# FFN rows split into fp16 halves in row layout and transposed by DMA instead of by TensorE

## The chip, the cores and the metric

One core of a Trainium2 chip runs the kernel. The metric is device time in microseconds, the median of several executions; the time before is 355.26 us (3 runs, 355.12 to 355.71). TensorE (PE) multiplies and, with an identity as the other operand, transposes 128x128 blocks into PSUM; VectorE (DVE), ScalarE (ACT) and GpSimd (POOL) do the element-wise work; SyncE (SP) only issues DMAs here.

## The reference, cut to what matters

`x`, `cond` and `ctx` are 8 items of 256 rows of 256 numbers (`cond` one row per item). First comes a slot attention of three rounds, then the feed-forward part (FFN) that the change is in. Everything is float32.

```python
x = x + xcond(cond, ctx, layernorm(x), ...)      # keys and values from ctx, 3 rounds of
                                                 # attention + MLP over 256 slots
x = x + ffn(layernorm(x), W_fc, ln_w, ln_b, W_proj)

def ffn(x, W_fc, ln_w, ln_b, W_proj):            # W_fc (1024, 256), W_proj (256, 1024)
    h = einsum('btd,hd->bth', x, ternary(W_fc))  # ternary: -1, 0 or 1 per weight
    h = gelu(h)
    h = (h - mean(h)) * rsqrt(var(h) + 1e-5) * ln_w + ln_b
    return einsum('bth,dh->btd', h, ternary(W_proj))
```

## The kernel before

All data stay in SBUF after the loads at the start. Each engine runs its own instruction stream, written out by hand; they meet at semaphores, and a waiting instruction holds all behind it on its engine. The first part prepares keys and values (up to about 50 us), the second is the three rounds (to about 280 us, the FFN's first items enter near its end), the third is the FFN, 8 items (b = 0 to 7) of two row tiles of 128 rows (rt = 0, 1); r = 2b + rt numbers the 16 row tiles. A buffer for items has two slots, u = b % 2.

The ternary weights are exact in fp16, and the other operand is split into a high fp16 half and the rest, a low fp16 half; both are multiplied, so a product costs two fp16 passes instead of a float32 one. The path of an item b through the FFN, with the functions' names:

- `stats_f` (DVE, `BATCH_NORM_STATS2` and `AGGREGATE`, L304 and L312) and `ln_coef` (POOL): mean and 1/sigma of each row. `apply_f` (DVE, L770): the normalised rows into `XR`, a part of the tile `PR`, float32, 128 partitions x (2 row tiles x 256).
- `rows_t` (PE, L351): four 128x128 transposes of `XR` into `ps_t[0]`.
- `copy_high` (ACT, L566): the transposed rows to fp16, `XTh`. `low_parts` (DVE, L777): the float32 transposed rows less `XTh`, `XTl`. Both lie in the memory of the tile `V`, which the FFN reuses; so do `GTh` and `GTl`.
- `fc` (PE, L1061): first-layer products of row tile r, 8 matmuls of 512 columns into `ps_mid`; at rt = 0 it waits for `low_parts` of its item. `gelu_half` (ACT, L572, into a part of `KT`); `centre` (DVE, first L784 the mean, then L790 two halves); `square_half` (ACT, L580); `rstd_g` (POOL).
- `hidden_t` (PE, L1075): eight transposes of the centred hidden row tile into `ps_low`; `high_half` (ACT, L587) and `low_half` (DVE, L799) split them; `proj` (PE, L1085): second-layer products, 16 matmuls of 256 columns into `ps_t`; `result` (DVE, L807): scale and add to `X`. The store (SP, L401) follows when both row tiles of the item are done.

The steps are shifted against each other. While PE does `fc` of row tile r it does `hidden_t` of r-1 and `proj` of r-2 right behind it: in item b, at rt = 0, the order is `fc(2b)`, `hidden_t(2b-1)`, `rows_t(b+1)`, `proj(2b-2)`; at rt = 1 `fc(2b+1)`, `hidden_t(2b)`, `proj(2b-1)`. DVE's order at rt = 0 is `stats_f(b+2)`, `centre(2b)`, `result(2b-2)`, `low_half(2b-1)`, `low_parts(b+1)`, and at rt = 1 `centre(2b+1)`, `result(2b-1)`, `low_half(2b)`, `apply_f(b+2)`. ACT's at rt = 0 is two gelus, two `high_half`, two squares, `copy_high(b+1)`.

Of the kernel before, what the change touches and what calls it, by code (L numbers as in the profile page):

```python
# [27 lines left out]
P = 128  # L28
# [28 lines left out]
def build(nc, x, ctx_in, w_nat, w_tr, w_fc_t, w_proj_t, cols, rows, out):  # L57
    with ExitStack() as stack:
# [67 lines left out]
        XR = PR[:, 0:2]  # L126
        vf = V[:, :, :, :].rearrange("p b j d -> p (b j d)")
# [10 lines left out]
        XTh = halves(0, 2 * C2 * N).rearrange("p (u c k) -> p u c k", u=2, c=C2)  # L138
        XTl = halves(C2 * N, 2 * C2 * N).rearrange("p (u c k) -> p u c k", u=2, c=C2)
# [70 lines left out]
        xth_ready = sem("xth_ready")  # L210
        xtl_ready = sem("xtl_ready")
# [79 lines left out]
        def ring(t, half, b):  # L291

            return t * STEPS + (B + half * B + b)

# [83 lines left out]
        @block.sync  # L378
        def _(sp):
            def load(dst, src, s, b):  # L380
                if b >= 2:
                    sp.wait_ge(s[b % 2], 16 * (b // 2))
                sp.dma_start(flat(dst, b), src[b]).then_inc(s[b % 2], 16)


            load(S, c_v, ctx_in_sem, 0)
            load(S, c_v, ctx_in_sem, 1)
            sp.wait_ge(wk_in, 16)
            for b in range(B):
                load(X, x_v, x_in_sem, b)  # L390
                if b + 2 < B:
                    load(S, c_v, ctx_in_sem, b + 2)
            sp.dma_start(wn[:, W1:W2 + 1].rearrange("p w c d -> p w (c d)"),
                         w_nat[3:5].rearrange("w p n -> p w n")).then_inc(mlp_in, 16)
            sp.dma_start(rowv[:, ROWS_EARLY:], rows[ROWS_EARLY:].rearrange("(a n) -> a n", a=1)
                         .broadcast_to([P, NROW - ROWS_EARLY])).then_inc(rows_in, 16)
            sp.dma_start(wf[:, 0:C2 * H], w_fc_t).then_inc(ffn_in, 16)
            sp.dma_start(wf[:, C2 * H:], w_proj_t).then_inc(ffn_in, 16)
            with sp.Fori(0, B) as b:
                sp.wait_ge(o_done, 2 * b + 2)  # L400
                sp.dma_start(o_v[b], flat(X, b)).then_inc(stored, 16)  # L401
            sp.wait_ge(stored, 16 * B)
# [118 lines left out]
        def _(act):  # L521
# [40 lines left out]
            def copy_high(b, u):  # L562
                act.wait_ge(t_ready, b + (T_FFN + 1))
                if not early(b):
                    act.wait_ge(f1_ready, 4 * b - 4)
                act.activation(XTh[:, u].rearrange("p c k -> p (c k)"), ps_t[0][:], ACT.Copy).then_inc(xth_ready, 1)  # L566
# [101 lines left out]
        def _(dve):  # L668
# [96 lines left out]
            def apply_f(b, u):  # L765
                dve.wait_ge(lnf.coef, b + 1)
                if not early(b):
                    dve.wait_ge(t_ready, b + (T_FFN - 1))  # L768
# [4 lines left out]
            def low_parts(b, u):  # L773
                dve.wait_ge(xth_ready, b + 1)
                if not early(b):
                    dve.wait_ge(f1_ready, 4 * b - 4)
                dve.tensor_tensor(XTl[:, u].rearrange("p c k -> p (c k)"), ps_t[0][:],  # L777
                                  XTh[:, u].rearrange("p c k -> p (c k)"), ALU.subtract).then_inc(xtl_ready, 1)
# [199 lines left out]
        def _(pe):  # L978
# [64 lines left out]
            def rows_t(b, u):  # L1043
                pe.wait_ge(xf_ready, 2 * b + 2)
                if isinstance(b, int) and b == 0:
                    pe.wait_ge(t_copied, T_FFN + RING)
                else:
                    pe.wait_ge(xtl_ready, b)
                blocks_t(pe, ps_t[0], XR[:, u])

            def fc(b, u, r, rt):
                if rt == 0:
                    pe.wait_ge(xtl_ready, b + 1)
                for h in range(2):
# [5 lines left out]
                    for k, (c, part) in enumerate(parts):  # L1060
                        last = pe.matmul(ps_mid[h][:], part[:, u, c, rt * P:(rt + 1) * P],  # L1061
# [27 lines left out]
            def ffn(b, u, rt, last=None):  # L1089
# [5 lines left out]
                if rt == 0 and (last is None or last < B - 1):  # L1095
                    rows_t(b + 1, 1 - u)
# [3 lines left out]
            def into_ffn(s):  # L1100
# [12 lines left out]
                if s == STEPS - 1:  # L1113
                    rows_t(0, 0)
# [87 lines left out]
```

## Time and profile before

| | |
|---|---|
| median of 3 runs | 355.26 us |
| profiled execution, span | 353.3 us |
| PE busy | 318.4 us (90%), of weights' loads 259.6 us beside it |
| DVE busy | 280.1 us (79%) |
| ACT busy | 241.1 us (68%) |
| POOL busy | 242.3 us (69%) |
| DMA | 13.20 MB, nearly all in the first 40 us |

The profile gives the profiled execution by its span, 353.3 us, and no other time of its own; what the median has more, 1.96 us, lies around the span. PE's matmuls are pipelined, so each group's listed time is some 0.16 us longer than the distance to the next group. Of the chain of waits that ended last, the FFN's PE lines are the largest parts (L1085 3%, L1061 2%); it reaches back to 319 us only. The FFN's items follow each other every 9.54 us in the steady part.

### The profile page before, as it was taken

Reading aid. Unit: us, or ns where it says so; the run is one execution under the profiler, and the core shown is the slowest. Engines: PE = TensorE matmul, PEld = TensorE weight load, DVE = VectorE, ACT = ScalarE, POOL = GpSimd, SP = SyncE. Lnnn points to the kernel's source line nnn. Section 1 sums busy time; section 2 is a strip of 40 time slices with the busy share of each in tenths; the row PEclk is TensorE's granted clock in tenths of the full one; section 3 lists DMA queues with packets and bytes.
Section 4 is the critical chain, followed back from the end, with each engine's and each line's share of the span. In section 5 each row is a group of like instructions: output and inputs, shape, how many; then the busy total and the mean of one; then the engine's idle time right before and its main releaser. Section 6 shows DMA issues by size and latency. Waiting matters only on the chain. (4 is left out here: it accounts for less than half of the span.)

```text
span 353.3 us, 7208 instructions
## 1 busy us (share of the span) xinstructions
PE 318.4 (90%) x1758; PEld 259.6 (73%) x1758; DVE 280.1 (79%) x849; ACT 241.1 (68%) x563; POOL 242.3 (69%) x529
## 2 busy tenths in 40 slices
PE   7997799999898888998989788999997599999995
PEld 7876687888786666777867676888874367777774
DVE  3699876899668779686697698896699889999874
ACT  2267786956856687757567977575548768888881
POOL 4278888267678888847688888668586985555331
PEclk9999999999999999999999999999999789999999
DMA  8997000000000000000000000000000000000001
GB/s 290 308 326 299 0 1 0 2 2 1 2 2 0 1 2 1 3 1 1 0 0 1 0 0 1 0 2 2 0 1 0 3 31 26 6 30 30 32 30 59
DMA packets 5312, 13.20 MB, mean 37 GB/s; under 512 B 673, under 2 KB 673, under 8 KB 4897
## 3 DMA queue, kind: packets, MB, share of 16 engines
q1 hardware_dynamic: 4160, 10.88, 8.6%
q10 hardware_dynamic: 1120, 1.98, 1.5%
q8 instruction: 10, 0.16, 0.2%
q14 instruction: 22, 0.17, 0.2%
HBM read 10.76 MB, written 2.10 MB: 36 GB/s over the span
## 5 line engine op out<-in xcount | busy, mean ns | idle before, releaser
L359 PE MATMUL ps_mid<-XT,wt 128*128 128x256 f32 x192 | 45.7, 381 | 2.9 <-ACT XT L370 2.9
L359 PE MATMUL ps_low<-V,PR 128*128 128x257 f32 x192 | 45.8, 381 | 0.5 <-DVE PR L882 0.5
L359 PE MATMUL ps_mid<-XT,KT 128*128 128x256 f32 x192 | 45.5, 380 | 0.6 <-ACT XT L370 0.6
L359 PE MATMUL ps_low<-wn,GT 128*128 128x256 f32 x192 | 45.2, 379 | 0.0
L335 ACT ACTIVATE XH<-S,lnp_ab 128x256 f32<-128x256 f32 x48 | 26.2, 593 | 24.0 <-POOL lnp_ab L329 23.9
L351 PE MATMUL ps_t<-ident,XH 128*128 128x128 f32 x192 | 29.7, 278 | 13.3 <-ACT XH L335 13.1
L335 ACT ACTIVATE XH<-S,lnm_ab 128x256 f32<-128x256 f32 x48 | 26.2, 595 | 22.0 <-POOL lnm_ab L329 22.0
L359 PEld LDWEIGHTS ps_low<-V,PR 128*128 128x128 f32 x192 | 36.3, 190 | 5.9 <-DVE PR L882 0.9
L359 PEld LDWEIGHTS ps_low<-wn,GT 128*128 128x128 f32 x192 | 36.4, 190 | 4.9
L359 PEld LDWEIGHTS ps_mid<-XT,wt 128*128 128x128 f32 x192 | 34.6, 190 | 7.3 <-ACT GT L650 2.3
L351 PEld LDWEIGHTS ps_t<-ident,XH 128*128 128x128 f32 x192 | 22.5, 141 | 23.2 <-ACT XH L335 12.3
L359 PEld LDWEIGHTS ps_mid<-XT,KT 128*128 128x128 f32 x192 | 34.6, 190 | 4.5 <-ACT XT L370 0.8
L370 ACT ACTIVATE XT<-ps_t 128x512 f32<-128x512 f32 x56 | 32.9, 588 | 4.4 <-PE ps_t L351 4.4
L506 POOL TENSOR_TENSOR S<-S,rowv 128x256 f32<-128x256 f32 x48 | 34.1, 732 | 0.0
L1085 PE MATMUL ps_t<-w,V 128*128 128x256 f16 x256 | 32.1, 282 | 0.9 <-DVE V L799 0.9
L1061 PE MATMUL ps_mid<-w,V 128*128 128x512 f16 x128 | 30.6, 382 | 0.8 <-ACT KT L572 0.7
L920 DVE TENSOR_TENSOR S<-ps_low,S 128x512 f32<-128x512 f32 x24 | 16.5, 687 | 18.1 <-PE ps_low L359 12.0
L1085 PEld LDWEIGHTS ps_t<-w,V 128*128 128x128 f16 x256 | 25.8, 101 | 4.6 <-DVE V L799 1.2
L790 DVE SCALAR_TENSOR_TENSOR KT<-KT,gneg,rowv 128x512 f32<-128x512 f32 x32 | 27.6, 904 | 1.0
L647 ACT ACTIVATE PR<-ps_mid,nmax 128x256 f32<-128x256 f32 x48 | 22.0, 461 | 8.4 <-DVE nmax L892 8.1
L580 ACT ACTIVATE XH<-KT,gneg 128x512 f32<-128x512 f32 x32 | 22.9, 723 | 5.2 <-DVE gneg L784 5.2
L572 ACT ACTIVATE KT<-ps_mid 128x512 f32<-128x512 f32 x32 | 19.0, 594 | 8.3 <-PE ps_mid L1061 7.2
(135 smaller groups left out, 743.4 us busy)
## 6 DMA issues: line engine op xcount, KB each, us to landing
S<-ctx SPq DMA_DIRECT2D x8, 256.0 KB, 3.8
X<-x SPq DMA_DIRECT2D x8, 256.0 KB, 3.8
out<-X SPq DMA_DIRECT2D x8, 256.0 KB, 2.0
rowv<-rows SPq DMA_DIRECT2D x1, 1920.0 KB, 9.9
wf<-w_fc_t SPq DMA_DIRECT2D x1, 1024.0 KB, 11.7
wf<-w_proj_t SPq DMA_DIRECT2D x1, 1024.0 KB, 13.6
wt<-w_tr ACTq DMA_DIRECT2D x1, 512.0 KB, 4.2
wn<-w_nat ACTq DMA_DIRECT2D x1, 512.0 KB, 5.7
```

The lines of the kernel that those rows point to most:

```text
L335: last = act.activation(dst[:, j], src[:, j], ACT.Identity, bias=ln.ab[:, at, 1, j:j + 1], scale=ln.ab[:, at, 0, j:j + 1])
L351: last = pe.transpose(dst[:, c * K + j * P:c * K + (j + 1) * P], src[:, j, c * P:(c + 1) * P], ident[:])
L359: last = pe.matmul(dst(m), lhs_t[:, c, m * P:(m + 1) * P], rhs[:, c, 0:n], start=(c == 0), stop=(c == 1))
L370: act.activation(XT[:, u].rearrange("p c k -> p (c k)"), ps_t[u][:], ACT.Copy).then_inc(t_copied, 1)
L506: pool.tensor_tensor(S[:, b, j], S[:, b, j], cond_row[:, b], ALU.add)\
L572: act.activation(Gf[:, rt, h * HALF:(h + 1) * HALF], ps_mid[h][:], ACT.Gelu, accum_out=gsum[:, rt, h:h + 1]).then_inc(gelu_done, 1)
L580: act.activation(flat(XH, 2 * rt + h), Gf[:, rt, h * HALF:(h + 1) * HALF], ACT.Square, bias=gneg[:, rt:rt + 1], accum_out=qsum[:, rt, h:h ...
L647: act.activation(dst[:, b % 4, j], src, ACT.Exp, bias=nmax[:, b, j:j + 1], accum_out=rsum[:, b, j:j + 1]).then_inc(mid_read, 1)
L790: dve.scalar_tensor_tensor(out=GC[:, rt, h * HALF:(h + 1) * HALF], in0=Gf[:, rt, h * HALF:(h + 1) * HALF], scalar=gneg[:, rt:rt + 1], in1= ...
L920: dve.tensor_tensor(flat(S, b), ps[:, 0], flat(S, b), ALU.add).then_inc(low_read, 2)
L1061: last = pe.matmul(ps_mid[h][:], part[:, u, c, rt * P:(rt + 1) * P], WfT[:, c, h * HALF:(h + 1) * HALF], start=(k == 0), stop=(k == 3))
L1085: last = pe.matmul(ps[:, 0:D], part[:, rt, k], WpT[:, k], start=(k == 0 and part is GTh), stop=(k == HT - 1 and part is GTl))
```

## The change

The split comes ahead of the transpose. `copy_high` and `low_parts` stay where they are in ACT's and DVE's order, but read the rows `XR` in SBUF and write the fp16 halves `XRh` and `XRl` in row layout (the other two quarters of `PR`). SP then issues two transposing DMAs for each item, fp16, each 128 partitions x 512 elements into 4 blocks of 128x128, straight into `XTh` and `XTl`, whose layout is now row tile, then column block. `fc` at rt = 0 waits for both (`xt_in`). `rows_t` is gone from PE. SP's loop of stores is written out, with the transposes for item b ahead of the store of item b-2.

```diff
--- before.py
+++ after.py
@@ -124,6 +124,12 @@
         GC = KT[:, :, :, :].rearrange("p b c n -> p (b c n)")[:, 2 * H:4 * H].rearrange("p (r h) -> p r h", r=2)
 
         XR = PR[:, 0:2]
+
+        def half_words(t, n):
+            return t.rearrange("p j k -> p (j k)").bitcast(F16).rearrange("p (u j d) -> p u j d", u=n, j=J2)
+
+        XRh = half_words(PR[:, 2], 2)
+        XRl = half_words(PR[:, 3], 2)
         vf = V[:, :, :, :].rearrange("p b j d -> p (b j d)")
 
         def halves(at, n):
@@ -135,8 +141,8 @@
         gneg = sb("gneg", [2])
         grstd = sb("grstd", [2, 3])
 
-        XTh = halves(0, 2 * C2 * N).rearrange("p (u c k) -> p u c k", u=2, c=C2)
-        XTl = halves(C2 * N, 2 * C2 * N).rearrange("p (u c k) -> p u c k", u=2, c=C2)
+        XTh = halves(0, 2 * C2 * N).rearrange("p (u j c k) -> p u j c k", u=2, j=J2, c=C2)
+        XTl = halves(C2 * N, 2 * C2 * N).rearrange("p (u j c k) -> p u j c k", u=2, j=J2, c=C2)
         GTh = halves(2 * C2 * N, 2 * HT * P).rearrange("p (r t k) -> p r t k", r=2, t=HT)
         GTl = halves(2 * C2 * N + HT * P, 2 * HT * P).rearrange("p (r t k) -> p r t k", r=2, t=HT)
 
@@ -207,8 +213,9 @@
         lnb_copied = sem("lnb_copied")
         x1_ready = sem("x1_ready")
         x1_shifted = sem("x1_shifted")
-        xth_ready = sem("xth_ready")
-        xtl_ready = sem("xtl_ready")
+        xrh_ready = sem("xrh_ready")
+        xrl_ready = sem("xrl_ready")
+        xt_in = [sem(f"xt_in{u}") for u in range(2)]
         f1_ready = sem("f1_ready")
         gelu_done = sem("gelu_done")
         gneg_ready = sem("gneg_ready")
@@ -291,6 +298,10 @@
         def ring(t, half, b):
 
             return t * STEPS + (B + half * B + b)
+
+        def xt_landed(b, u):
+
+            return 16 * b + (32 - 16 * u)
 
         T_FFN = B + ROUNDS * STEPS
 
@@ -396,9 +407,22 @@
                          .broadcast_to([P, NROW - ROWS_EARLY])).then_inc(rows_in, 16)
             sp.dma_start(wf[:, 0:C2 * H], w_fc_t).then_inc(ffn_in, 16)
             sp.dma_start(wf[:, C2 * H:], w_proj_t).then_inc(ffn_in, 16)
-            with sp.Fori(0, B) as b:
-                sp.wait_ge(o_done, 2 * b + 2)
-                sp.dma_start(o_v[b], flat(X, b)).then_inc(stored, 16)
+            def rows_t(b):
+                u = b % 2
+                sp.wait_ge(xrh_ready, b + 1)
+                sp.wait_ge(xrl_ready, b + 1)
+                if b >= 2:
+                    sp.wait_ge(f1_ready, 4 * b - 4)
+                for dst, src in ((XTh, XRh), (XTl, XRl)):
+                    sp.dma_start_transpose(dst[:, u].rearrange("p j c k -> p (j c) k"),
+                                           src[:, u].rearrange("p j d -> p (j d)")).then_inc(xt_in[u], 16)
+
+            for b in range(B + 2):
+                if b < B:
+                    rows_t(b)
+                if b >= 2:
+                    sp.wait_ge(o_done, 2 * b - 2)
+                    sp.dma_start(o_v[b - 2], flat(X, b - 2)).then_inc(stored, 16)
             sp.wait_ge(stored, 16 * B)
 
         @block.gpsimd
@@ -560,10 +584,11 @@
             pairs(act, prologue)
 
             def copy_high(b, u):
-                act.wait_ge(t_ready, b + (T_FFN + 1))
+                act.wait_ge(xf_ready, 2 * b + 2)
                 if not early(b):
-                    act.wait_ge(f1_ready, 4 * b - 4)
-                act.activation(XTh[:, u].rearrange("p c k -> p (c k)"), ps_t[0][:], ACT.Copy).then_inc(xth_ready, 1)
+                    act.wait_ge(xt_in[u], xt_landed(b - 2, u))
+                act.activation(XRh[:, u].rearrange("p j d -> p (j d)"), XR[:, u].rearrange("p j d -> p (j d)"),
+                               ACT.Copy).then_inc(xrh_ready, 1)
 
             def gelu_half(r, rt, h):
                 act.wait_ge(f1_ready, 2 * r + (h + 1))
@@ -765,17 +790,18 @@
             def apply_f(b, u):
                 dve.wait_ge(lnf.coef, b + 1)
                 if not early(b):
-                    dve.wait_ge(t_ready, b + (T_FFN - 1))
+                    dve.wait_ge(xrh_ready, b - 1)
+                    dve.wait_ge(xrl_ready, b - 1)
                 for j in range(J2):
                     dve.tensor_scalar(XR[:, u, j], X[:, b, j], lnf.mv[:, u, j, 0:1], lnf.ab[:, u, 0, j:j + 1],
                                       ALU.subtract, ALU.mult).then_inc(xf_ready, 1)
 
             def low_parts(b, u):
-                dve.wait_ge(xth_ready, b + 1)
+                dve.wait_ge(xrh_ready, b + 1)
                 if not early(b):
-                    dve.wait_ge(f1_ready, 4 * b - 4)
-                dve.tensor_tensor(XTl[:, u].rearrange("p c k -> p (c k)"), ps_t[0][:],
-                                  XTh[:, u].rearrange("p c k -> p (c k)"), ALU.subtract).then_inc(xtl_ready, 1)
+                    dve.wait_ge(xt_in[u], xt_landed(b - 2, u))
+                dve.tensor_tensor(XRl[:, u].rearrange("p j d -> p (j d)"), XR[:, u].rearrange("p j d -> p (j d)"),
+                                  XRh[:, u].rearrange("p j d -> p (j d)"), ALU.subtract).then_inc(xrl_ready, 1)
 
             def centre(r, rt):
                 dve.wait_ge(gelu_done, 2 * r + 2)
@@ -1040,17 +1066,9 @@
             pe.wait_ge(low_read, 2 * (B - 1) + 2 * RING)
             column(ps_low[0][:, 1], wn[:, W1], lambda c: col("lnm_b", c)).then_inc(w_prod, 1)
 
-            def rows_t(b, u):
-                pe.wait_ge(xf_ready, 2 * b + 2)
-                if isinstance(b, int) and b == 0:
-                    pe.wait_ge(t_copied, T_FFN + RING)
-                else:
-                    pe.wait_ge(xtl_ready, b)
-                blocks_t(pe, ps_t[0], XR[:, u])
-
             def fc(b, u, r, rt):
                 if rt == 0:
-                    pe.wait_ge(xtl_ready, b + 1)
+                    pe.wait_ge(xt_in[u], xt_landed(b, u))
                 for h in range(2):
                     if isinstance(r, int) and r == 0:
                         pe.wait_ge(mid_read, 2 * T_FFN + 2 * RING)
@@ -1058,7 +1076,7 @@
                         pe.wait_ge(gelu_done, 2 * r + (h - 1))
                     parts = [(c, part) for c in range(C2) for part in (XTh, XTl)]
                     for k, (c, part) in enumerate(parts):
-                        last = pe.matmul(ps_mid[h][:], part[:, u, c, rt * P:(rt + 1) * P],
+                        last = pe.matmul(ps_mid[h][:], part[:, u, rt, c],
                                          WfT[:, c, h * HALF:(h + 1) * HALF], start=(k == 0), stop=(k == 3))
                     last.then_inc(f1_ready, 1)
 
@@ -1092,8 +1110,6 @@
                 fc(b, u, r, rt)
                 if rt == 1 or not first:
                     hidden_t(r - 1, 1 - rt)
-                if rt == 0 and (last is None or last < B - 1):
-                    rows_t(b + 1, 1 - u)
                 if not first:
                     proj(r - 2, rt)
 
@@ -1110,8 +1126,6 @@
                     pe.wait_ge(lnb_copied, 1)
                     pe.matmul(ps_low[0][:, 1, D:2 * D], ones[0:1, :], lnb_row[0:1, :], start=True, stop=True)\
                       .then_inc(lnb_prod, 1)
-                if s == STEPS - 1:
-                    rows_t(0, 0)
                 if s in (FFN_STEP, FFN_STEP + 1):
                     ffn(0, 0, s - FFN_STEP)
```

SP's queue from the last load on, before: one loop with the stores. `PR` holds the rows and their halves, `V` the transposed halves.

```order
L398 DMA wf<-w_proj_t 128x2048
L399 UNCONDITIONAL_BRANCH
L399 ISA
L401 ISA [waits o_done]
L401 DMA out<-X 128x512
L399 REGISTER_ALU
L399 COMPARE_AND_BRANCH
```

The same place now, items 0 to 3 of the transposes:

```order
L409 DMA wf<-w_proj_t 128x2048
L417 DMA_TRANSPOSE V<-PR 128x4x128 [waits xrl_ready,xrh_ready]
L417 DMA_TRANSPOSE V<-PR 128x4x128
L417 DMA_TRANSPOSE V<-PR 128x4x128 [waits xrl_ready,xrh_ready]
L417 DMA_TRANSPOSE V<-PR 128x4x128
L417 DMA_TRANSPOSE V<-PR 128x4x128 [waits f1_ready,xrl_ready,xrh_ready]
L417 DMA_TRANSPOSE V<-PR 128x4x128
L425 DMA out<-X 128x512 [waits o_done]
L417 DMA_TRANSPOSE V<-PR 128x4x128 [waits f1_ready,xrl_ready,xrh_ready]
L417 DMA_TRANSPOSE V<-PR 128x4x128
L425 DMA out<-X 128x512 [waits o_done]
```

The queue gains 16 transposing DMAs, two for each item, each pair behind a wait for both halves; from item 2 on also for the products that read the slot before, and a store stands behind each such pair.

PE's order from the first-layer products of item 6, before (`ps_mid` takes `fc`, `ps_low` `hidden_t`, `ps_t` `rows_t` and `proj`):

```order
L1061 MATMUL ps_mid<-w,V 128x512 [waits gelu_done,xtl_ready]
L1061 MATMUL ps_mid<-w,V 128x512 x3
L1061 MATMUL ps_mid<-w,V 128x512 [waits gelu_done]
L1061 MATMUL ps_mid<-w,V 128x512 x3
L1075 MATMUL ps_low<-ident,KT 128x128 [waits gtl_ready,gc_done]
L1075 MATMUL ps_low<-ident,KT 128x128 x3
L1075 MATMUL ps_low<-ident,KT 128x128 [waits gtl_ready,gc_done]
L1075 MATMUL ps_low<-ident,KT 128x128 x3
L351 MATMUL ps_t<-ident,PR 128x128 [waits xtl_ready,xf_ready]
L351 MATMUL ps_t<-ident,PR 128x128 x3
L1085 MATMUL ps_t<-w,V 128x256 [waits o_done,gtl_ready]
```

The same place now:

```order
L1079 MATMUL ps_mid<-w,V 128x512 [waits gelu_done,xt_in0]
L1079 MATMUL ps_mid<-w,V 128x512 x3
L1079 MATMUL ps_mid<-w,V 128x512 [waits gelu_done]
L1079 MATMUL ps_mid<-w,V 128x512 x3
L1093 MATMUL ps_low<-ident,KT 128x128 [waits gtl_ready,gc_done]
L1093 MATMUL ps_low<-ident,KT 128x128 x3
L1093 MATMUL ps_low<-ident,KT 128x128 [waits gtl_ready,gc_done]
L1093 MATMUL ps_low<-ident,KT 128x128 x3
L1103 MATMUL ps_t<-w,V 128x256 [waits o_done,gtl_ready]
```

The four transposes of `PR` are gone, the second-layer products follow the hidden layer's transposes directly, and the item's first product waits for the DMA's semaphore `xt_in0` instead of DVE's `xtl_ready`. DVE's and ACT's orders keep their sequence.

## Rows read from the trace of the kernel before

**Rows 1.** Busy time in one item of the FFN: start:end, length, then each engine's, granted clock, DMA

```profile
308.88:318.42 9.54, 9.35 (x69) 6.93 (x68) 9.19 (x20) 8.10 (x23) 4.93 (x9) 1.00 0.07 27
```

**Rows 2.** Timeline of PE, one item: start, length, what, [idle before]

```profile
307.15 1.89 PE L1061 MATMUL ps_mid<-w,V 128*128 128x512 f16 x8
...
310.11 0.66 PE L351 MATMUL ps_t<-ident,PR 128*128 128x128 f32 x4 [0.19 <-DVE PR L770]
310.60 1.91 PE L1085 MATMUL ps_t<-w,V 128*128 128x256 f16 x16
312.35 1.89 PE L1061 MATMUL ps_mid<-w,V 128*128 128x512 f16 x8
...
314.95 1.91 PE L1085 MATMUL ps_t<-w,V 128*128 128x256 f16 x16
316.69 1.89 PE L1061 MATMUL ps_mid<-w,V 128*128 128x512 f16 x8
```

**Rows 3.** Timeline of DVE, items 0 to 2

```profile
260.93 0.66 DVE L777 TENSOR_TENSOR V<-ps_t,V 128x512 f16<-128x512 f32 x1
...
271.17 0.68 DVE L777 TENSOR_TENSOR V<-ps_t,V 128x512 f16<-128x512 f32 x1
...
281.28 2.43 DVE L790 SCALAR_TENSOR_TENSOR KT<-KT,gneg,rowv 128x512 f32<-128x512 f32 x2
283.98 0.48 DVE L807 SCALAR_TENSOR_TENSOR X<-ps_t,grstd,X 128x256 f32<-128x256 f32 x1 [0.27 <-PE ps_t L1085]
...
285.58 0.68 DVE L777 TENSOR_TENSOR V<-ps_t,V 128x512 f16<-128x512 f32 x1
```

**Rows 4.** Timeline of PE, items 1 and 2, and item 7's first product

```profile
279.41 1.12 PE L351 MATMUL ps_t<-ident,PR 128*128 128x128 f32 x4 [2.75 <-DVE PR L770]
280.32 3.62 PE L1085 MATMUL ps_t<-w,V 128*128 128x256 f16 x16
...
288.45 1.89 PE L1061 MATMUL ps_mid<-w,V 128*128 128x512 f16 x8
...
335.76 1.89 PE L1061 MATMUL ps_mid<-w,V 128*128 128x512 f16 x8
```

**Rows 5.** Timeline of ACT, the item of rows 2

```profile
311.34 0.72 ACT L580 ACTIVATE XH<-KT,gneg 128x512 f32<-128x512 f32 x1 [0.60 <-DVE gneg L784]
...
312.77 0.57 ACT L566 ACTIVATE V<-ps_t 128x512 f16<-128x512 f32 x1
...
319.11 0.20 ACT L572 ACTIVATION_READ_ACCUMULATOR KT<-ps_mid 128x1 f32 x1
319.21 1.08 ACT L587 ACTIVATE V<-ps_low 128x512 f16<-128x512 f32 x2
```

**Rows 6.** Timeline of DVE, the item of rows 2

```profile
311.09 0.21 DVE L784 TENSOR_SCALAR gneg<-gsum 128x1 f32<-128x1 f32 x1
...
312.68 0.48 DVE L807 SCALAR_TENSOR_TENSOR X<-ps_t,grstd,X 128x256 f32 x1
313.08 1.28 DVE L799 TENSOR_TENSOR V<-ps_low,V 128x512 f16<-128x512 f32 x2
314.27 0.68 DVE L777 TENSOR_TENSOR V<-ps_t,V 128x512 f16<-128x512 f32 x1
```

**Rows 7.** The page's groups of instructions: busy, mean ns | idle before

```profile
L790 DVE SCALAR_TENSOR_TENSOR KT<-KT,gneg,rowv 128x512 f32<-128x512 f32 x32 | 27.6, 904 | 1.0
```

**Rows 8.** DMA issues (KB each, us to landing), and the stores' issues on SP (ns)

```profile
S<-ctx SPq DMA_DIRECT2D x8, 256.0 KB, 3.8
out<-X SPq DMA_DIRECT2D x8, 256.0 KB, 2.0
L401 SPq DMA_DIRECT2D out<-X x8: 338/339/362, 289.3 to 350.9; - x8
```

**Rows 9.** Timeline of ACT, item 0

```profile
266.79 0.57 ACT L572 ACTIVATE KT<-ps_mid 128x512 f32<-128x512 f32 x1
```

**Rows 10.** Busy time and granted clock around the fall of TensorE's clock

```profile
278.00:279.40 1.40, 0.00 (x0) 0.00 (x0) 0.78 (x3) 1.38 (x4) 1.32 (x3) 0.50 0.00 0
```

## The prediction

> **What bounds the kernel now.** I read the busy shares of the engines first (table of the profile section), and then went straight to the last stage, because the diff changes nothing before it. The stage does eight items of 256 rows; each item is two row tiles, and r = 2b + rt numbers them. The view of busy time by stretch, cut at the starts of one item's first-layer products, shows a period of 9.54 us in which PE is busy 9.35 and DVE 9.19 [rows 1]. Both look full, so the question is which one would keep the period if the other were relieved. The timeline of PE over one item [rows 2] gives its own work: the reader is to see that from a first-layer group (312.35) to the second-layer group behind it (314.95) pass 2.60 us, with the hidden layer's eight transposes in between, and 1.74 us more to the next first-layer group (316.69); that is 4.34 us per row tile, 8.68 per item. The other 0.86 us of the period are the changed transposes: from 307.15 to 310.60 pass 3.45 us where the tile without them takes 2.60, since PE waits 0.19 us for VectorE's rows and then spends 0.49 us until the next group starts. So PE has 0.86 us of removable work per item, but VectorE has only 9.54 - 9.19 = 0.35 us of air [rows 1]: a PE that is 0.86 us shorter can shorten the period by 0.35 us at most.
>
> **What the change removes.** On PE, 8 groups of four transposes with their waits. They don't carry the sum: of the last stage's handovers the steady ones are worth 0 to 0.35 us each (above), and only while the data come in time. In item 1 VectorE's first result waits 0.27 us for a second-layer group [rows 3] that stands behind the transposes on PE (those waited 2.75 us for rows [rows 4]); I give that 0.27 us back. copy_high and low_parts keep their place on ACT and DVE, but read SBUF instead of PSUM. For ACT, 0.57 us now against 0.72 us of a same-size ACT instruction that reads SBUF [rows 5], +0.15 at most; in the cycle below it has 0.3 us of cover. For DVE, 0.68 us [rows 6]; another 128x512 instruction with SBUF operands means 0.904 us over the kernel [rows 7], where some run beside GpSimd's additions. Between 0 and +0.22 us, taken as 0, since VectorE will be waiting anyway; if it were not, it would be 6 x 0.22 = 1.3 us, which I keep for the range.
>
> **What it adds.** Per item two transposing DMAs of 128 KB each on SP's queue, and a path that did not exist: low_parts ends, SP is released, two transfers are issued and both must land before PE may start the item's first product (the wait on xt_in). On PE everything of the next item stands behind that wait: the hidden-layer transposes of r-1, the second-layer products of r-2, and so VectorE's result for r-2, which stands in front of its low halves and of the next low_parts. Call the time from the end of low_parts to the first product L. The trace has the two instructions with nothing but PE between them: low_parts ends at 314.95 [rows 6] and the product starts at 316.69 [rows 2], a window of 1.74 us.
>
> The cycle with this path is, counted from an item's first product: 2.60 us to the second-layer group; its matmuls 1.91 us, then 0.17 us until VectorE's result starts (310.60 + 1.91 = 312.51, result at 312.68) [rows 2, 6]; 0.40 us to the low halves, 1.19 us to low_parts, 0.68 us for it [rows 6]. Sum 6.95 us, and the period becomes 6.95 + L once that is more than VectorE's 9.2 to 9.5. Two side branches fit under it: the second gelu is read out at 319.11 + 0.20 - 316.69 = 2.62 us after the first product [rows 2, 5], VectorE then takes 312.68 - 311.09 = 1.59 us [rows 6] to the result, ready at 4.3 against the 4.68 at which the second-layer group lets it go; and ACT's copy ends about 5.8 us in (2.62, then the two high halves 1.08, the two squares 312.77 - 311.34 = 1.43, itself 0.57 to 0.72) [rows 5], against 6.27 when low_parts starts.
>
> L is what the trace doesn't show. Bounds: a plain 256 KB store lands 2.0 us after its issue, and an issue occupies SP 0.339 us [rows 8]. If the two halves together behave as that one store, with the second issued 0.34 us later and 0.1 us for the semaphores, L = 2.4. If each costs what the loads of 256 KB took under full DMA load, 3.8 us [rows 8], one after the other, L = 7.6. Nearest is the store, an idle queue in this same stage. I take L = 4.0, two store-like transfers end to end: every row that a transpose writes is gathered from 128 source partitions, where the store copies rows as they are, and nothing in the trace shows two such transfers overlapping. The Trainium skill ("DMA: Bandwidth & Descriptors", the table on fast hardware descriptor generation, column of previous generations) counts 262,144 sequencer cycles for an SBUF to SBUF transpose of 8,192 tiles, 32 a tile; these are 64 tiles of 16 x 128, 2,048 cycles, 1.7 us at the 1.2 GHz that "Trainium Kernel Development and Optimization" (NeuronCore Architecture) gives for SyncE; with the store's 2.0 us that estimate is L = 3.7, which would give 362.5 us. No row here shows a transposing DMA.
>
> **The sum.** Handovers 0 and 1 have other work over them. Item 0: low_parts ends at 261.59 [rows 3], the product could start at 265.6, its first half is done half of 1.89 us later [rows 2], and the gelu can start at some 266.7; now it starts at 266.79, behind other work of ACT [rows 9]. Item 1: low_parts ends at 271.85, product at 275.85, gelus read out at 278.5; VectorE uses them at 281.28 [rows 3]. Cost 0 for both. Item 2: low_parts ends at 285.58 + 0.68 - 0.27 = 285.99, the product starts at 285.99 + L instead of 288.45 [rows 3, 4]: L - 2.46. From item 2's product to item 7's there are five periods: now 335.76 - 288.45 = 47.31 [rows 4], then 5 x (6.95 + L) = 34.75 + 5L. Behind item 7's product nothing changes. Together: L - 2.46 + 34.75 + 5L - 47.31 = 6L - 15.0 us. With L = 4.0 this is +9.0. The profiled execution's span is 353.3 us; the median of the runs is 355.26, 1.96 more, for what lies around the span, which I leave as it is: 362.3 + 1.96 = 364.3 us.
>
> **The rivals.**
> A, the transposes land in time. At L = 2.4 the formula gives -0.6, and below that VectorE's own 9.2 us takes over, so the best case is 6 x -0.35 = -2.1: 353.2 to 355.3 us, say 354.4. It decides at L = 2.5. For it: the DMA engines are idle in this stage but for the stores, and the store's 256 KB in 2.0 us. Against it: 1.74 us of window, and two issues. The Trainium skill ("Advanced Engine Details and Errata", X-Bar Transpose) says that transpose DMAs are as fast as regular ones; by that rule L would be the store's, 2.4, and the change would come out at 354.7 us. No row here tests it.
> B, the transposing DMA is much slower than a copy, by its many small pieces or by a descriptor cost on SP: L = 6 to 7.6, 6L - 15.0 = +21 to +31, 376 to 386 us. For it: nothing in this trace has such pieces, so nothing excludes it.
> C, TensorE's clock falls in the new waits. At L = 4.0 PE idles 10.95 - 8.68 = 2.3 us in one piece per item. In this trace a gap of 2.75 us after a stretch of shorter gaps left the clock at 0.50 (1.2 GHz) [rows 10], and the second-layer group behind it took 3.62 us instead of 1.91 [rows 2, 4]. The groups on the cycle's path (first-layer, hidden, second-layer, 4.5 us) would lose up to 1.7 us in that group and as much in the others: with a fall in every second item some 3 x 3.5 = 10 us more, 375 us. Against it: the gap is shorter and the rest of the item is dense work.
>
> **How the numbers follow.** Forecast (L from 2.6 to 5.5, 356 to 373) 0.60; A 0.18; B 0.12; C 0.10. The predicted time is the forecast's 364.3. The range takes the whole of the forecast, the upper half of A and the near part of B and C: 354.6 to 377. A change of 0.2% (0.7 us) is what a measurement of this kernel can tell: faster needs L below 2.4 and air on VectorE, 0.10; within 0.2%, L of 2.4 to 2.6, 0.08; slower 0.82.
>
> **What would show it.** In the profile after: PE idle before the first-layer product of items 2 to 7, released by a DMA of about 4 - 1.7 = 2.3 us each; a period of about 11 us instead of 9.54, PE and DVE both below 90% in it; ACT's gelu and DVE's centring late by the same. VectorE's wait before the result instruction behind a second-layer group, a tenth or two. The landing time of the transposes in the list of DMA issues gives L directly. Wrong would be: a period of 9.2 to 9.5 (A), a landing above 5 us (B), or granted clock below 1.00 between 290 and 340 us (C).

## The result and the profile after

The changed kernel takes 367.89 us (median of 4 executions, 365.12 to 369.79) against 355.19 us of the kernel before in the same comparison (4 executions, 354.70 to 355.71). The ratio is 1.0346, interval 1.0295 to 1.0398: 12.7 us slower. The forecast was +9.0 us, 364.3 us, in a range of 354.6 to 377. The profiled execution took 367.16 us, its span 364.6 us against 353.3, which is +11.3 us.

The page shows the wait and where it sits. `L1079` is the first-layer product (before: `L1061`), `L1103` the second-layer one.

```profile
PEclk9999999999999999999999999999988988999999
...
L1079 PE MATMUL ps_mid<-w,V 128*128 128x512 f16 x128 | 35.1, 424 | 17.9 <-DMA V<-PR 17.9
...
L1103 PE MATMUL ps_t<-w,V 128*128 128x256 f16 x256 | 30.8, 275 | 1.3 <-DVE V L825 1.3
```

The first group now has 17.9 us of idle time ahead of it, all released by the DMA into `V`, 8 times. The mean of one of its matmuls went from 382 to 424 ns, although their shape did not change, and the granted clock is below full in four slices, where it was in two before.

Busy time by item, cut at each item's first product, items 2 to 6. The columns are those of [rows 1].

```profile
290.22:302.74 12.52, 10.56 (x65) 6.96 (x65) 8.91 (x19) 8.03 (x21) 5.07 (x11) 0.86 0.15 42
302.74:315.16 12.42, 10.53 (x65) 7.56 (x65) 9.32 (x20) 8.24 (x21) 4.70 (x10) 0.86 0.15 42
315.16:325.99 10.83, 8.87 (x65) 6.42 (x65) 9.46 (x20) 8.00 (x21) 4.83 (x10) 1.00 0.18 51
325.99:336.64 10.65, 8.86 (x64) 6.41 (x65) 9.22 (x20) 8.00 (x21) 4.67 (x10) 1.00 0.17 46
336.64:347.26 10.62, 8.87 (x64) 6.42 (x65) 8.46 (x16) 7.92 (x21) 3.75 (x8) 1.00 0.18 50
```

The last three periods are 10.83, 10.65 and 10.62 us where they were 9.54 [rows 1]; PE is busy 8.86 or 8.87 us in each (82 to 84%), its own work without the transposes. The first two are 12.5 us and have a mean clock of 0.86. The timeline of PE shows the two kinds of item:

```profile
290.22 3.51 PE L1079 MATMUL ps_mid<-w,V 128*128 128x512 f16 x8 [2.41 <-DMA V<-PR]
293.52 1.16 PE L1093 MATMUL ps_low<-ident,KT 128*128 128x128 f32 x8
294.51 1.91 PE L1103 MATMUL ps_t<-w,V 128*128 128x256 f16 x16
...
325.99 1.90 PE L1079 MATMUL ps_mid<-w,V 128*128 128x512 f16 x8 [1.96 <-DMA V<-PR]
327.72 1.04 PE L1093 MATMUL ps_low<-ident,KT 128*128 128x128 f32 x8
328.59 1.91 PE L1103 MATMUL ps_t<-w,V 128*128 128x256 f16 x16
...
336.64 1.90 PE L1079 MATMUL ps_mid<-w,V 128*128 128x512 f16 x8 [1.79 <-DMA V<-PR]
...
347.26 1.90 PE L1079 MATMUL ps_mid<-w,V 128*128 128x512 f16 x8 [1.75 <-DMA V<-PR]
```

In the item at 325.99 the distances between groups (1.73, 0.87 us) are those of [rows 2], and the 1.96 us ahead of it are the new wait. In the item at 290.22 the first-layer group takes 3.51 us instead of 1.90.

The chain of waits, in order of time, gives the new path of one item; pieces called "issue" and one of 0.02 us are left out:

```profile
330.65 0.08 DVE X L833
...
332.25 0.69 DVE PR L803
332.99 1.20 SPq L417
334.23 2.37 DMA V<-PR
336.64 1.90 PE ps_mid L1079 x8
```

And VectorE's rows for the same item, to be held against [rows 6]:

```profile
328.74 0.21 DVE L810 TENSOR_SCALAR gneg<-gsum 128x1 f32<-128x1 f32 x1 [0.82 <-ACT KT L597]
...
330.65 0.48 DVE L833 SCALAR_TENSOR_TENSOR X<-ps_t,grstd,X 128x256 f32 x1 [0.25 <-PE ps_t L1103]
331.05 1.28 DVE L825 TENSOR_TENSOR V<-ps_low,V 128x512 f16<-128x512 f32 x2
332.25 0.68 DVE L803 TENSOR_TENSOR PR<-PR 128x512 f16<-128x512 f32 x1
```

VectorE waits 0.82 us for the gelu ahead of `gneg`, 0.25 us for the second-layer group ahead of its result, and ends the low half (`PR<-PR`) at 332.93. SP issues from 332.99; the second issue starts at 334.23, lands 2.4 us later, and PE starts at 336.64.

### The profile page after: what moved, and what is told of

Its sections match the earlier page's. It is cut to its first block and busy times, and to the rows that moved or that the text cites. A ratio compares the mean times of both kernels' runs of the same rounds, so it can differ in the third digit from the quotient of the medians.

```text
span 364.6 us, 7111 instructions
## 1 busy us (share of the span) xinstructions
PE 319.0 (87%) x1726; PEld 258.5 (71%) x1726; DVE 281.5 (77%) x849; ACT 241.1 (66%) x563; POOL 242.4 (66%) x529
## 5 line engine op out<-in xcount | busy, mean ns | idle before, releaser
L1079 PE MATMUL ps_mid<-w,V 128*128 128x512 f16 x128 | 35.1, 424 | 17.9 <-DMA V<-PR 17.9
L370 PEld LDWEIGHTS ps_low<-wn,GT 128*128 128x128 f32 x192 | 37.2, 194 | 5.5 <-issue 0.3
L1079 PEld LDWEIGHTS ps_mid<-w,V 128*128 128x128 f16 x128 | 12.7, 105 | 34.1 <-issue 13.3
L1103 PE MATMUL ps_t<-w,V 128*128 128x256 f16 x256 | 30.8, 275 | 1.3 <-DVE V L825 1.3
L816 DVE SCALAR_TENSOR_TENSOR KT<-KT,gneg,rowv 128x512 f32<-128x512 f32 x32 | 28.2, 922 | 1.0
L1103 PEld LDWEIGHTS ps_t<-w,V 128*128 128x128 f16 x256 | 25.1, 99 | 4.7 <-DVE V L825 1.8
L461 POOL TENSOR_SCALAR grstd<-qsum 128x1 f32<-128x1 f32 x16 | 5.5, 345 | 33.2 <-DVE X L833 33.2
```

Source lines behind the costliest of these rows:

```text
L370: last = pe.matmul(dst(m), lhs_t[:, c, m * P:(m + 1) * P], rhs[:, c, 0:n], start=(c == 0), stop=(c == 1))
L816: dve.scalar_tensor_tensor(out=GC[:, rt, h * HALF:(h + 1) * HALF], in0=Gf[:, rt, h * HALF:(h + 1) * HALF], scalar=gneg[:, rt:rt + 1], in1= ...
L1079: last = pe.matmul(ps_mid[h][:], part[:, u, rt, c], WfT[:, c, h * HALF:(h + 1) * HALF], start=(k == 0), stop=(k == 3))
L1103: last = pe.matmul(ps[:, 0:D], part[:, rt, k], WpT[:, k], start=(k == 0 and part is GTh), stop=(k == HT - 1 and part is GTl))
```

## The experiments

All times are medians, ratios against the kernel before on the same chip. "Period" is the time from one item's first product to the next.

**1. Each half's transfer waits for its own half only.** SP's waits are changed, nothing else.

```diff
-                sp.wait_ge(xrh_ready, b + 1)
-                sp.wait_ge(xrl_ready, b + 1)
                 if b >= 2:
                     sp.wait_ge(f1_ready, 4 * b - 4)
-                for dst, src in ((XTh, XRh), (XTl, XRl)):
+                for dst, src, made in ((XTh, XRh, xrh_ready), (XTl, XRl, xrl_ready)):
+                    sp.wait_ge(made, b + 1)
```

> Only SP's order of waits is changed: each half's transposing DMA is issued when its own half is ready, the high half's while VectorE still works. Theory (the path low_parts, SP's second issue 1.25 us, landing 2.4 us sets the period): the low half's DMA no longer stands behind the 1.25 us issue of the other, L falls from 3.8 to 2.55 us, the period from 10.7 to 9.5 us, PE waits about 0.6 us per item instead of 1.8 to 2, and by 6L - 15.0 the time is 355 to 356.5 us. Rival (the two transfers are bound by the DMA engines, not by the issue): the second still lands 3.8 us after low_parts or nearly, period above 10.3 us, time 363 to 367 us.

Measured: 356.60 us, ratio 1.0027 (1.0012 to 1.0042), 0.1 us above what was expected. PE's timeline at items 3 and 4, then the item between them:

```profile
297.83 1.90 PE L1078 MATMUL ps_mid<-w,V 128*128 128x512 f16 x8 [0.61 <-DMA V<-PR]
...
307.41 1.90 PE L1078 MATMUL ps_mid<-w,V 128*128 128x512 f16 x8 [0.72 <-DMA V<-PR]
```

```profile
297.83:307.41 9.58, 8.86 (x64) 6.43 (x65) 9.37 (x20) 8.00 (x21) 5.12 (x9) 1.00 0.20 56
```

The period is 9.58 us and the wait 0.6 to 0.7 us. From the end of the low half to the product pass 2.4 to 2.5 us instead of 3.7 to 3.9 (3.0 once, ahead of item 7), and the granted clock is 1.00 in all of items 2 to 6. So all but 1.0 of the 12.7 us go away when the low half's issue no longer stands behind the other: by 6L - 15.0 some 7.5 us for the 1.25 us of issue, and about 3.5 us of low clock, which does not come with these shorter waits. The rival is out.

**2. Both halves made earlier.** `copy_high(b+1)` moves up behind ACT's two gelus, `low_parts(b+1)` ahead of `centre` on VectorE; the waits of SP stay as in the changed kernel.

```diff
                 gelu_half(r, rt, 1)
+                if rt == 0 and (last is None or last < B - 1):
+                    copy_high(b + 1, 1 - u)
...
+                if rt == 0 and (last is None or last < B - 1):
+                    low_parts(b + 1, 1 - u)
                 centre(r, rt)
```

(Not shown: both calls are taken away from their old places.)

> The transposes are the same, but both halves are made earlier: copy_high directly behind the item's two gelus on ACT, low_parts ahead of centre on DVE. low_parts then ends some 4.9 us ahead of the next item's first product instead of 1.7 us. Theory (latency L = 3.8 us on the path is the whole loss): no wait for the DMA on PE in items 2 to 7, the period is VectorE's, 9.2 to 9.5 us, clock 1.00, time 353 to 355 us, at or a little below before. Rival (transposing DMAs also cost by contention in SBUF, or the row-layout halves cost ACT and DVE more): period 9.7 us or more with no DMA wait, time 357 us or more.

Measured: 356.14 us, ratio 1.0012 (0.9994 to 1.0029). Items 2, 3 and 4:

```profile
289.17:298.94 9.77, 9.69 (x66) 6.68 (x64) 8.84 (x19) 7.64 (x20) 5.40 (x10) 0.92 0.20 55
298.94:308.64 9.70, 8.86 (x66) 6.44 (x64) 9.25 (x20) 8.19 (x22) 5.23 (x10) 1.00 0.20 56
308.64:317.92 9.28, 8.87 (x67) 6.46 (x65) 8.51 (x19) 8.03 (x22) 5.84 (x10) 1.00 0.20 57
```

PE waits for no DMA from item 2 on, at a DMA share of 0.20. The periods of items 2 and 3 are still 9.77 and 9.70 us; only from item 4 on are they 9.28, 9.27 and 9.07. So the latency on the path was nearly the whole loss. The total missed the expected 353 to 355 us: item 2's product came at 289.17 us, 0.7 us later than in the kernel before [rows 4]. In item 1 the low half now stands ahead of VectorE's centring, which starts at 282.09 us (281.26 in experiment 1); PE idles 2.23 us for it and runs at a clock of 0.50 from 285.00 to 289.17:

```profile
285.78 3.60 PE L1103 MATMUL ps_t<-w,V 128*128 128x256 f16 x16 [0.47 <-DVE V L825]
```

**3. The change without its transfers.** SP issues the transposing DMAs of items 0 and 1 only; items 2 to 7 multiply those rows again.

```diff
-                if b < B:
+                if b < 2:
                     rows_t(b)
...
-                    pe.wait_ge(xt_in[u], xt_landed(b, u))
+                    pe.wait_ge(xt_in[u], 32)
```

(`copy_high` and `low_parts` wait for 32 too.)

> Leaves out the transposing DMAs of items 2 to 7 (these items multiply the transposed rows of items 0 and 1 again); every other instruction stays. It shows what the rest of the change is worth without the DMA: theory: VectorE-bound, period 9.2 to 9.5 us, items 0 and 1 still wait 3 us each, 353 to 355 us. Rival (PE was the bound, not DVE): period 8.7 to 8.9 us, 350 to 352 us. The difference to the kernel with the earlier halves is what the transfers cost other engines, 0 by the theory.

Measured: 354.56 us, ratio 0.9972 (0.9956 to 0.9989). So taking 0.86 us per item off PE is worth 1 us in all. The five periods are 8.95, 9.65, 9.65, 9.66 and 9.06 us, together 46.97 against 47.31 before: in the middle of the stage they are longer than the 9.54 us before.

```profile
305.93:315.58 9.65, 9.04 (x67) 6.41 (x64) 9.44 (x20) 7.91 (x23) 5.11 (x10) 1.00 0.07 27
```

9.65 us, with VectorE busy 9.44 of it. VectorE's centring pair and, beside it, GpSimd's addition, one fence each:

```profile
304.88 2.36 DVE L816 SCALAR_TENSOR_TENSOR KT<-KT,gneg,rowv 128x512 f32<-128x512 f32 x2
```

```profile
304.76 1.26 POOL L479 TENSOR_TENSOR X<-X,lnb_out 128x512 f32 x1
```

The pair takes 2.36 us; clear of the addition, the same pair takes 1.42 us (for instance at 301.11 in this profile). In the kernel before, with another overlap, it took 2.01 us:

```profile
315.34 2.01 DVE L790 SCALAR_TENSOR_TENSOR KT<-KT,gneg,rowv 128x512 f32<-128x512 f32 x2
```

The expectation took the difference between this kernel and the one of experiment 2 for what the transfers cost the other engines, 0 by the theory. It is 1.6 us. But the two also differ in item 2's late product and in where the addition falls, and no run has one order with and without transfers; what the transfers cost others is not isolated.

**4. The same, with GpSimd's addition cut to one column.** All but one of the addition's 512 columns are left out.

```diff
-                    pool.tensor_tensor(flat(X, b), flat(X, b), lnb_out[:]..., ALU.add)
+                    pool.tensor_tensor(flat(X, b)[:, 0:1], flat(X, b)[:, 0:1], lnb_out[:, 0, 0:1], ALU.add)
```

> As the kernel without the transposing DMAs of items 2 to 7, and GpSimd's addition of the bias rows (128 x 512, once per item) does one column only, so the rest of that addition is left out. Theory (VectorE keeps the period, and its centring pair takes 2.36 instead of 1.42 us because GpSimd's addition runs beside it on the same SBUF): the pair takes 1.42 us, the period falls from 9.65 to 8.7 to 8.9 us where PE is the bound, time 350 to 352 us. Rival (the pair is slow for another reason, or another engine keeps the period): pair 2.0 us or more, time within 1 us of 354.6.

Measured: 351.13 us, ratio 0.9861 (0.9838 to 0.9883). The pair, and the period:

```profile
304.47 1.42 DVE L815 SCALAR_TENSOR_TENSOR KT<-KT,gneg,rowv 128x512 f32<-128x512 f32 x2
```

```profile
305.52:314.27 8.75, 8.75 (x66) 6.46 (x64) 8.54 (x20) 7.91 (x23) 4.03 (x9) 1.00 0.08 30
```

1.42 us, and PE is now busy for the whole period of 8.75 us, 0.07 more than the 8.68 us of its own work in the prediction. This shows what bound the stage in experiment 3: VectorE together with GpSimd's addition, not PE.

**5. One transposing DMA per item instead of two.** The halves of an item lie side by side, and one DMA of 128 x 1024 elements takes both.

```diff
-                for dst, src in ((XTh, XRh), (XTl, XRl)):
-                    sp.dma_start_transpose(dst[:, u]..., src[:, u]...).then_inc(xt_in[u], 16)
+                sp.dma_start_transpose(XTa[:, u]..., XRa[:, u]...).then_inc(xt_in[u], 16)
```

(Not shown: the new layout of the two buffers, and the semaphore's counts, which change here and in experiment 6.)

> One transposing DMA of 128 x 1024 elements (64 tiles of 16 x 128) per item instead of two of 32 tiles; the halves of an item lie side by side. Theory (SP's 1.25 us of issue go by tiles): issue about 2.5 us, data landed 3.6 to 3.8 us after low_parts as now, 366 to 368 us. Rival (the issue is a fixed price of the instruction): issue 1.25 us, L = 2.6 us, period 9.5 to 9.6 us, 355 to 357 us.

**6. Four DMAs per item**, one for each row tile of each half.

```diff
                 for dst, src in ((XTh, XRh), (XTl, XRl)):
-                    sp.dma_start_transpose(dst[:, u]..., src[:, u]...).then_inc(xt_in[u], 16)
+                    for j in range(J2):
+                        sp.dma_start_transpose(dst[:, u, j], src[:, u, j]).then_inc(xt_in[u], 16)
```

> Four transposing DMAs of 128 x 256 (16 tiles each) per item instead of two of 32. Theory (issue by tiles with a small fixed part): issue 0.6 to 0.8 us each, 2.5 to 3.2 us together, L = 3.8 to 4.4 us, 367 to 371 us. Rival (fixed price of the instruction): 1.25 us each, L = 6.3 us, by 6L - 15.0 it is +23 us, 378 us or more.

Measured: one DMA 360.18 us, ratio 1.0137 (1.0096 to 1.0178); four DMAs 395.34 us, ratio 1.1123 (1.1094 to 1.1153). The instructions on `PR` in the changed kernel, then the transposes with one and with four DMAs (ns min/median/max of an issue; landing counted from the start of the issue):

```profile
L417 SPq DMA_TRANSPOSE V<-PR x16: 1190/1262/1272, 262.0 to 344.8; - x16
L590 ACT ACTIVATE PR<-PR x8: 614/624/633, 259.0 to 341.5; 128x512 f16<-128x512 f32 x8
L803 DVE TENSOR_TENSOR PR<-PR x8: 660/682/683, 261.2 to 342.8; 128x512 f16<-128x512 f32 x8
```

```profile
L416 SPq DMA_TRANSPOSE V<-PR x8: 1232/1237/1313, 261.6 to 335.4; - x8
...
DMA to landing us min/median/max: 2.7/2.8/3.4
```

```profile
L418 SPq DMA_TRANSPOSE V<-PR x32: 1168/1246/1283, 261.6 to 371.0; - x32
...
DMA to landing us min/median/max: 2.3/2.4/3.1
```

My theory for these two was wrong, and the one DMA also missed the rival's 355 to 357 us. An issue costs SP 1.24 us for 64 tiles, 1.26 for 32 and 1.25 for 16: it is a price of the instruction, not of the tiles. Only the landing grows a little, 2.4 to 2.8 us. In the one-DMA kernel the product follows the low half by 318.75 - 315.76 = 2.99 us, and the period of that item is 9.95 us. The four-DMA kernel has 312.19 - 305.78 = 6.41 us. By 6L - 15.0 that makes +2.9 and +23.5 us against measured +4.6 and +39.8 us. For the one DMA, the profiled execution (358.80 us) fits, its span is 3.0 us longer than before; two of the four executions took 361.6 and 362.3 us, at a lower mean clock (0.985 and 0.986 instead of 0.990). For the four, PE's first group takes 3.4 to 3.6 us in every item, and in the five periods from item 2's product PE is busy 55.3 us where 5 x 8.87 = 44.4 would be its time at full clock: 11 of the missing 16 us. The rest was not traced.

**7. PE kept busy ahead of the wait.** Eight unused matmuls into a free PSUM bank.

```diff
                 if rt == 0:
+                    for _ in range(8):
+                        pe.matmul(ps_t[0][:], WfT[:, 0, 0:P], WfT[:, 0, 0:HALF], start=True, stop=True)
                     pe.wait_ge(xt_in[u], xt_landed(b, u))
```

> The changed kernel with 8 unused fp16 matmuls of 512 columns on PE (1.73 us) ahead of each wait for the transposes, into a PSUM bank that is free. Theory (3 to 4 us of the loss are TensorE's clock at 1.2 GHz behind the waits in items 0 to 3): granted clock 1.00 in the whole last stage, all periods 10.6 to 10.9 us, time 363 to 365 us, with less spread between executions. Rival (the slower matmuls lie in the waits' shadow, the 12.5 us periods come from something else): 12.5 us periods stay, 367 to 369 us.

Measured: 364.52 us (364.07 to 365.09), ratio 1.0252 (1.0229 to 1.0274), 3.4 us less than the changed kernel and a spread of 1.0 us instead of 4.7. The stage from 290 us on:

```profile
290.00:345.00 55.00, 52.96 (x360) 36.04 (x360) 45.62 (x91) 39.94 (x105) 23.31 (x46) 1.00 0.18 49
```

Clock 1.00, periods of 10.63 to 10.83 us but for one: item 3 came 11.88 us after item 2, where one issue on SP took 2.24 us instead of 1.2. That is not explained. Before 290 us the clock still fell once (0.94 in the mean).

**8. The two useful edits together.** Edit 1, and edit 2 only from item 2 on (`not early(b)` on the new places, `early(b)` on the old ones).

> The two earlier edits together: each half's transposing DMA waits for its own half only, and copy_high and low_parts are made earlier, but only from item 2 on (in items 0 and 1 they keep their place, since the earlier low_parts delayed item 1 and its first-layer product of item 2 came at 289.2 us instead of 288.4). Theory: item 2's product at 288.3 to 288.5 us, then periods of 9.3 to 9.5, 9.3, 9.3, 9.3 and 9.1 us without waits for the DMA, item 7's product at about 334.9 us, span 352.2 us, ratio to before 0.996 to 0.998. Rival (what the earlier order lost in items 1 to 3 comes back in another place): ratio 1.000 or more.

Measured: 354.80 us, ratio 0.9972 (0.9959 to 0.9985). This is the one version with the full computation that beats both kernels, the kernel before by 0.7 us. Item 2's product came at 289.12 us and not at the expected 288.3 to 288.5, but this execution ran 0.5 us behind the profiled one of the kernel before already before the FFN. The five periods are 8.99, 9.27, 9.29, 9.27 and 9.08 us, together 45.90 against 47.31. It ran a second time beside experiment 9:

> The best version again on the same chip as the control, so that the two can be compared. Expected as measured: ratio 0.996 to 0.998.

354.63 us, ratio 0.9973 (0.9957 to 0.9990). The item from 307.38:

```profile
307.38:316.67 9.29, 8.87 (x67) 6.46 (x65) 8.51 (x19) 8.04 (x22) 5.84 (x10) 1.00 0.20 56
```

**9. The order alone, with TensorE still transposing.** On the kernel before, from item 2 on `copy_high(b+1)` behind the gelus and `low_parts(b+1)` behind the centring.

```diff
                 centre(r, rt)
+                if rt == 0 and (last is None or last < B - 1) and not early(b):
+                    low_parts(b + 1, 1 - u)
                 if not first:
                     result(b - 1, r - 2, rt)
```

(Not shown: `copy_high`, moved in the same way, and the old places.)

> A control on the kernel before, TensorE still transposing: from item 2 on copy_high stands directly behind the item's gelus on ACT and low_parts directly behind the centring on DVE. It asks whether the earlier halves alone are worth something, without the DMA. Theory (the gain of the best version needs PE free of the 0.86 us of transposes and their wait; the order alone moves nothing off an engine): ratio 0.999 to 1.004, 355 to 357 us, period 9.5 to 9.7 us. Rival (the order alone moves GpSimd's addition off VectorE's centring and brings the gain): ratio 0.997 or less, period 9.3 us or less.

Measured: 358.41 us, ratio 1.0083 (1.0051 to 1.0116), so the earlier halves are a loss without the DMA, and a larger one than I expected. PE's transposes and VectorE's centring in this kernel, then VectorE in the kernel of experiment 8:

```profile
310.07 0.65 PE L351 MATMUL ps_t<-ident,PR 128*128 128x128 f32 x4 [0.59 <-DVE PR L772]
```

```profile
315.35 2.43 DVE L792 SCALAR_TENSOR_TENSOR KT<-KT,gneg,rowv 128x512 f32<-128x512 f32 x2
```

```profile
305.73 1.42 DVE L817 SCALAR_TENSOR_TENSOR KT<-KT,gneg,rowv 128x512 f32<-128x512 f32 x2
307.70 0.48 DVE L834 SCALAR_TENSOR_TENSOR X<-ps_t,grstd,X 128x256 f32 x1 [0.56 <-PE ps_t L1106]
```

With PE transposing, the period is 10.0 us: the rows arrive 0.59 us late for PE, and the addition of GpSimd lies over the second centring pair (2.43 us). In the best version that pair takes 1.42 us in items 2 to 5 (2.43 in item 6) and VectorE then waits 0.56 us for PE. `low_parts` stands in different places in the two (behind and ahead of the centring), so how much of the difference is the place of the low half, and with it where the addition falls, and how much PE's transposes is not separated.

## Why the prediction was right, point by point

**The mechanism and the cycle held.** I had said that the period becomes 6.95 + L, with L from the end of `low_parts` to the product. Measured from the product at 325.99 to the end of `low_parts` at 332.93: 6.94 us; from 336.64 to 343.48: 6.84 us. L is 332.93 to 336.64, 3.71 us; 3.88 and 3.78 us in the neighbours. I had taken 4.0. Experiments 1 and 2 take L down or off the path and nearly all of the loss goes. But one of my own signs of being wrong also came, the low clock of rival C: the time lies in the range by a cycle that held and a clock that was not in the sum.

**L was right for a partly wrong reason.** I had put it together as two landings of 2.0 us, end to end. It is two issues on SP, of which the first costs its full 1.24 us, and one landing of 2.4 us; the two landings do overlap. The lower bound, which took a store's 0.339 us for an issue [rows 8], was therefore out of reach for two DMAs: the price of an issue was the unknown to look for. Rival A's premise failed on both counts: 128 KB transposed land after 2.4 us where the store's 256 KB take 2.0, and the issue costs 1.25 us instead of 0.34. So a transposing DMA of this size is not as fast as a plain one. The Trainium skill's 262,144 sequencer cycles for 8,192 tiles ("DMA: Bandwidth & Descriptors", the table on fast hardware descriptor generation), from which I had worked out 32 for a tile and the estimate L = 3.7, came near by accident: experiments 5 and 6 show no price for a tile in the issue.

**The handover of item 2** was forecast at L - 2.46 = +1.54 us; the product came at 290.22 instead of 288.45, +1.77. Of this 0.29 us is no effect of the stage: the profiled execution is that much behind the one before already in the last round, as the same products of PE show, first before, then after:

```profile
251.45 1.89 PE L359 MATMUL ps_low<-wn,GT 128*128 128x256 f32 x8
```

```profile
251.74 1.89 PE L370 MATMUL ps_low<-wn,GT 128*128 128x256 f32 x8
```

At this place the other profiles lie between 0.4 us ahead of the kernel before and 0.5 us behind it, so positions in different profiles tell no less than that; periods and spans of a stage don't suffer from it. VectorE ended `low_parts` at 286.43 where I had 285.99, and most of this is the same 0.29 us.

**The zero for items 0 and 1** held, but in item 1 with little left. Its product came at 276.72 (I had 275.85) and took 3.55 us at a low clock instead of 1.89, so the second gelu was read out at 281.01 us, not at 278.5; VectorE used it at 281.51:

```profile
280.31 0.60 ACT L597 ACTIVATE KT<-ps_mid 128x512 f32<-128x512 f32 x1 [0.98 <-PE ps_mid L1079]
```

**The mis-sized term is the clock.** It stood among the rivals with a chance of 0.10 and not in the sum. Five periods were forecast at 54.75 us and took 57.04. At the 10.70 us of the last three they would have been 53.5; the other 3.5 us are the two items with clock 0.86. The granted clock around item 2's product, and in item 3:

```profile
288.00:290.20 2.20, 0.00 (x0) 0.00 (x0) 2.20 (x5) 0.11 (x2) 2.00 (x4) 1.00 0.41 97
290.20:292.00 1.80, 1.78 (x5) 0.72 (x6) 1.32 (x6) 0.00 (x0) 1.20 (x4) 0.54 0.35 130
...
304.00:306.00 2.00, 2.00 (x9) 1.46 (x8) 0.56 (x4) 1.26 (x4) 0.95 (x2) 0.50 0.03 8
```

PE was idle from 288.0 to 290.2, and the first group behind the gap ran at the lower of the two levels (0.50, 1.2 GHz) for most of 290.2 to 294. The gap ahead of item 2 was 2.41 us, and 1.96 us ahead of item 3; the later gaps of 1.75 to 1.96 us left the clock full, and so did one of 1.89 ahead of item 4. I had argued that 2.3 us was short beside the 2.75 us of the kernel before; the row did not support a bound between them. Rival C had the mechanism, but its price was too high: a fall costs 1.7 us (from the first product to the end of the low half 8.65 and 8.61 us instead of 6.94), not 3.5. Experiment 7 shows the size: 3.4 us. Its kernel takes 364.5 us, which is the forecast's 364.3, a sum without the clock. The spread of the changed kernel over 4.7 us fits too, though no run tests it alone: the mean clock is 0.981 in the two shorter executions and 0.977 in the two longer ones, and with the clock kept up the spread is 1.0 us.

The sum over the profiled execution: item 2's product +1.77, five periods +9.73 (57.04 - 47.31), behind item 7's product -0.20 (17.34 against 17.54), together +11.3 us, in which the 0.29 us from ahead of the stage is contained. Without the clock's 3.5 us it would be +7.8, which is 6 x 3.8 - 15.0.

**What the removal was worth** was forecast at 0 to 0.35 us per item. Experiment 3 gives 1 us for the whole kernel. But the air that I had read, 9.54 - 9.19, was not the limit it seemed, since VectorE's 9.19 us is no fixed amount of work: with other timing GpSimd's addition lay over the whole centring pair, and the period grew to 9.65, or shrank to 9.27 in experiment 8, where it did not.

**The two copies from SBUF.** ACT's took 0.624 us in the median (0.57 before; I had allowed up to 0.72), VectorE's 0.682 us as before (0.678). 0 was right.

## What to carry to other kernels

A DMA that replaces an engine's work adds a latency, and the place where the data are made must move up by that latency before anything is saved; read the window between producer and consumer first (here 1.74 us for a path of 3.8). At the sizes run here every transposing DMA costs its queue about 1.25 us whatever its size, so do not cut them small (four per item: 395.3 us), and let none wait for data that belong to another (one for both halves: 360.2 us; two, each behind its own half: 356.6 us). Where two engines both look full, ask what the second does when the first is relieved, and whether a third engine's work slides over it: here 0.86 us off PE per item brought 1 us in all.

## What the runs showed of the hardware that I had not expected

- Issuing a transposing DMA from SP: 1.17 to 1.31 us for 16, 32 or 64 tiles of 16 x 128 fp16 (one issue in experiment 7 took 2.24), against 0.34 us for a plain store of 256 KB. Landing 2.4 us from the start of the issue for 16 or 32 tiles, 2.8 us for 64.
- VectorE's pair of 128x512 float32 instructions on SBUF (L816): 1.42 us alone, 2.36 us beside GpSimd's 1.26 us addition on SBUF; where the addition started 0.8 us into the pair (experiment 8), the pair stayed at 1.42 us and GpSimd's took 1.74 us instead; where it started 0.1 us into it (experiment 9), both were long, 2.43 and 1.78 us.
- A clock of 0.50 behind a wait of 1.96 us in one item and a clock of 1.00 behind 1.96 us in another of the same kernel.
